# A two-layer attention and state-space block on one core: the front, gate, skip and second layer norm of all four items of a tile one step later

## What is computed

```python
# layer 0: attention between 4x4 blocks of pixels
x = x + attention(group_norm(x))
# layer 1: layer norm, a selective state-space scan on 4 chunks of 128 channels, layer norm, projection
xn = layer_norm(group_norm(x))            # 4096 positions, 512 channels
for chunk in 4 chunks of 128 channels:    # the "items" below
    xi, z = split(chunk @ in_proj.T)      # 256 + 256
    xc = silu(causal_conv4(xi) + conv_b)
    dt, B, C = split(xc @ x_proj.T)       # 8, 16, 16
    dt = softplus(dt @ dt_proj.T + dt_b)
    for position: h = exp(dt*A)*h + (dt*xc)*B ; y = sum_s h*C   # 16 states
    y = (y + xc*D) * silu(z)
    out_chunk = y @ out_proj.T + skip*chunk
out = x + layer_norm(all chunks) @ proj_w.T + proj_b
```

## Time and profile before

| what | value |
|---|---|
| median of 3 runs | 16086.48 us (16082.97 to 16089.99) |
| the profiled execution's own time | 16090.54 us |
| its span | 16088.7 us, mean granted clock of PE 0.947 |
| DVE busy | 14823.6 us (92%) |
| POOL busy | 14788.2 us (92%) |
| PE busy | 14186.2 us (88%) |
| ACT busy | 11509.9 us (72%) |
| windows 2, 3, 4, 5 of one ordinary tile (around 8.6 ms) | 61.74, 61.85, 58.54, 60.26 us |

### The profile page before, as it was taken

How to read it: one execution, slowest core, us unless ns; L and a number is a source line. 1 busy time by engine, 2 the same in 40 slices (tenths; PEclk the granted TensorE clock), 3 DMA queues, 4 the chain that set the end, 5 groups by cost and what they waited for, 6 DMA issues and landing times. The chain is left out here.

```text
span 16088.7 us, 151421 instructions
## 1 busy us (share of the span) xinstructions
PE 14186.2 (88%) x30720; PEld 5741.6 (36%) x30720; DVE 14823.6 (92%) x13024; ACT 11509.9 (72%) x18891; POOL 14788.2 (92%) x6275
## 2 busy tenths in 40 slices
PE   6988989889898898888889888899888898888888
PEld 2333333333333333333333333333333333333333
DVE  6999999999999999999999999999999999999998
ACT  5777767777677767777677776777767777677776
POOL 5999989999899989999899998999989999899998
PEclk8999999999999999999999999999999999999999
DMA  3444444444444444444444444444444444444444
GB/s 131 156 163 163 159 153 162 162 164 153 157 157 160 163 155 158 159 160 169 150 156 162 157 169 149 158 163 161 163 148 161 164 160 166 150 153 164 156 154 139
DMA packets 739082, 2537.63 MB, mean 158 GB/s; under 512 B 77241, under 2 KB 78017, under 8 KB 721729
## 3 DMA queue, kind: packets, MB, share of 16 engines
q1 hardware_dynamic: 738112, 2527.45, 46.1%
HBM read 2376.15 MB, written 150.99 MB: 157 GB/s over the span
## 5 line engine op out<-in xcount | busy, mean ns | idle before, releaser
L1460 POOL TENSOR_TENSOR RING<-RING,CS 128x1024 f32<-128x1024 f32 x4096 | 9597.9, 2363 | 1036.2 <-DVE RING L1150 973.3
L1150 DVE TENSOR_TENSOR_SCAN RING<-DA,HS,RING 128x512 f32<-128x512 f32 x8192 | 9946.1, 1265 | 496.9 <-ACT DA L777 451.1
L388 PE MATMUL YP<-RING,EYE 128*128 128x512 f32 x16384 | 8172.0, 632 | 1400.6 <-POOL RING L1460 1307.3
L777 ACT ACTIVATE DA<-ITEM,AN 128x512 f32<-128x512 f32 x8192 | 5495.8, 684 | 3017.5 <-DVE RING L1150 3001.5
L388 PEld LDWEIGHTS YP<-RING,EYE 128*128 128x128 f32 x16384 | 3126.8, 198 | 5995.0 <-issue 3596.3
L1130 DVE TENSOR_TENSOR RING<-DTP,BS 128x1024 f32<-128x1024 f32 x3072 | 3687.7, 1205 | 129.0 <-ACT DTP L847 117.6
L1447 POOL TENSOR_TENSOR RING<-ITEM,BS 128x1024 f32<-128x1024 f32 x1024 | 2421.3, 2365 | 10.0 <-DMA BS<-bc_rows 0.3
L388 PE MATMUL FL<-XN,WC 128*128 128x512 f32 x4096 | 1913.9, 611 | 9.8 <-ACT XN L866 4.6
L388 PEld LDWEIGHTS FL<-XN,WC 128*128 128x128 f32 x4096 | 821.4, 201 | 1087.4 <-issue 1079.1
L791 ACT ACTIVATE ITEM<-FL,COL 128x512 f32<-128x512 f32 x512 | 348.9, 682 | 1056.8 <-PE FL L388 1056.6
L388 PE MATMUL FL<-LS,WP 128*128 128x512 f32 x2048 | 983.2, 603 | 6.1 <-POOL LS L1482 6.1
(11 more groups left out here) (125 smaller groups left out, 10879.3 us busy)
## 6 DMA issues: line engine op xcount, KB each, us to landing
BS<-bc_rows SPq DMA_DIRECT2D x2048, 512.0 KB, 4.9
CS<-bc_rows SPq DMA_DIRECT2D x2048, 512.0 KB, 3.6
XR<-in_x SPq DMA_DIRECT2D x128, 1024.0 KB, 7.6
x_slices<-XR SPq DMA_DIRECT2D x64, 1024.0 KB, 8.3
XR<-x_slices SPq DMA_DIRECT2D x64, 1024.0 KB, 7.6
out<-XR SPq DMA_DIRECT2D x64, 1024.0 KB, 8.1
XR<-in_wqkv SPq DMA_DIRECT2D x24, 1024.0 KB, 7.8
bc_rows<-ROWS SPq DMA_DIRECT2D x256, 64.0 KB, 4.5
```

Source lines behind the costliest of these rows:

```text
L388: return pe.matmul(*a, **k)
L777: act.activation(DA[:, h, :], DT[:, i % 2, h, :], ACT.Exp, scale=AN[:, h, s:s + 1]).then_inc(dA_ready, 1)
L1150: dve.tensor_tensor_scan(H[:, slot(n), h, :], DA[:, h, :], U[:, slot(n), h, :], HS[:, i % ITEMS, h, s:s + 1], ALU.mult, ALU.add).then_inc( ...
L1460: pool.tensor_tensor(G[:, slot(n)], H[:, slot(n)], CS[:, s % C_ROWS, :].unsqueeze(1).broadcast_to([P, NH, T]), ALU.mult).then_inc(g_ready, 1)
```

## The change

d becomes 1 in every window. The two places that used d for another purpose keep their behaviour: `xi_first` stays at step 15 of the window before, except in window 3 and the `new` window (`conv_late`). The calls that did not go by d but touch the same PSUM banks are moved one step along with it: on PE the means of the second layer norm (window 4, steps 7 and 8 to 8 and 9) and the first block of the last projection (window 5, steps 6 and 7 to 7 and 8); on DVE the centring of the second layer norm (step 9 to 10) and the first `finish` (step 8 to 9). Whatever is at `s == k + d` moves on each engine: PE's second half of the convolution, z, dbc, both dt matmuls, the out projection and window 2's means; ACT's copies, silus, softplus pieces, group norm, square and rstd of the first layer norm; DVE's gate, skip, centring and scaling of the first layer norm, and the order of U 5 and 7; POOL's four dt operations. Not moved: ACT's skip term (12), `dtx_copy` (15), the square (11) and rstd (15) of the second layer norm, PE's d term (9), SP's queue.

```diff
         def late(j, new=False):
-            return 1 if j == 3 or new else 0
+            return 1
+
+        def conv_late(j, new=False):
+
+            return j == 3 or new
...
                     if front:
-                        if s == 0 and d:
+                        if s == 0 and conv_late(j, new):
                             front_left(tile, w)
...
                     if j == 0 and ln2:
-                        if s == 7:
+                        if s == 8:
                             pe.wait_ge(yb_ready, tile * ITEMS + w)
                             channel_mean(YB, mu2_ready, (0, 1))
-                        if s == 8:
+                        if s == 9:
                             channel_mean(YB, mu2_ready, (2, 3))
...
                     if j == 1 and ln2:
-                        if s == 6:
+                        if s == 7:
                             pe.wait_ge(yn_ready, ahead)
                             pe.wait_ge(yb_ready, tile * ITEMS + w)
                             proj(0, (0, 1))
-                        if s == 7:
+                        if s == 8:
                             proj(0, (2, 3))
...
-                    if j == 0 and ln2 and s == 9:
+                    if j == 0 and ln2 and s == 10:
                         centre(YB, mu2_ready, cen2_ready, ahead)
                     if j == 1 and ln2:
-                        for at, o in ((8, 0), (11, 1), (13, 2), (15, 3)):
+                        for at, o in ((9, 0), (11, 1), (13, 2), (15, 3)):
```

## The result

The changed kernel takes 16385.29 us (16379.01 to 16385.95, 4 runs) against 16084.72 us (16072.48 to 16089.99, 4 runs): the ratio is 1.0187, 95% interval 1.0169 to 1.0205. It is 300 us slower. The prediction was 16,110 us with a range of 16,045 to 16,185.

A forecast was written before the change was run, and what follows sets the result against it. DVE and POOL, each 92% busy, bound it by turns; only POOL's idle time counts. Window 4 +62, window 2 +25, special and first windows -63 make +24 on 16090.5, less 4.1 to the runs' median: 16,110 us, range 16,045 to 16,185.

The forecast's parts named there:

- slower, 0.40: Whole kernel: chance 0.40 that the change measures slower, against 0.45 same and 0.15 faster; a measurement tells 0.2%, 32 us.
- The gate's wait vanishes, the stall moves to scan 5: Early windows: DVE's gate wait for PE, 473 us, falls under 30; scan 5 waits instead, at +20.94 against +20.82.
- +18.67 without the gate's wait: Window 4 before the change: scan 5 would start 18.67 us after scan 0, not +20.82, if the gate did not wait.
- Window 4, +1.1: POOL's waits up to out 11 sum to 3.9 against 2.7 before; +1.1 us in each of 56 windows, +62.
- Window 5, 0: POOL is always behind DVE there and waits for nothing, so scan 5 coming 1.5 earlier is worth 0.
- over 150: Sign that the forecast is right: DVE waits for `dtx_copy` in over 150 windows.
- Window 2, +0.7: POOL waits 1.5 at out 10 against 0.80 before: +0.7 us in each of 35 windows, +25.
- Window 3, unchanged: Window 3 is unchanged and inherits the delay, since its convolution waits for out 14; priced at 0.
- The special windows, -57: Per image: tile 4's window 5 -4.4, the next +1.2, tile 5's window 5 with attention window -4.0, tile 6's window 4 -1.0.
- Slower by PE: Rival, chance 0.13: PE, nearly full in window 5, can't catch up; 57 windows 2 lose 1.5 each, +85, 16,195 us.
- Faster: z not held: Rival, chance 0.12: the gate does not hold z, or silu finds it ready; scan 5 1.2 earlier, -80, some 16,005 us.
- The C rows: Rival, chance 0.08: a C row lands 0.7 late at outs 7 to 10 in 64 windows 5, +45, 16,155 us.

The follow-up runs named there:

- e1: Changed kernel, but in windows 2, 4, 5 PE issues z before sum 0 instead of behind it: 16118.53 us, ratio 1.0021 to the kernel before.
- e7: Kernel before with one edit, PE issues the convolution's second half one step later, behind sum 15: 16165.61 us, ratio 1.0049 to the kernel before.
- e4: Changed kernel with z ahead of sum 0 and POOL's dt operations at their old steps, in windows 2, 4, 5: 15992.32 us, ratio 0.9946.
- e3: Changed kernel with POOL's four dt operations back at their old steps in windows 2, 4, 5: 16242.02 us, ratio 1.0103 to the kernel before.
- e2: Changed kernel with two extra matmuls on PE ahead of sum 0 in windows 2, 4, 5, result overwritten by z: 16300.91 us, ratio 1.0135.
- e12: Changed kernel with extra unread matmuls in ordinary windows 2, four ahead of sum 12 and five ahead of sum 13: 16379.79 us, ratio 1.0185.

## Why the prediction was wrong

The direction that I thought possible (slower, 0.40) came true, the size did not: +300 where +24 stood, outside the range.

Two steps failed. The length of sum 0 was taken from a row in which PE had hardly been idle, and put into windows where PE idles 2 us before it (window 5, 0 forecast, +49). And window 3 was put at nothing because its code is unchanged (+83): POOL's dt*x, moved behind out 12, was weighed against DVE's wait for its copy and not against PE's sums and the convolution behind them. The special windows, put at -57 (+36), met the slow sum 0 as well, lost more to z's order than was forecast, and have a part that stays open. Term by term:

**The gate's wait vanishes, the stall moves to scan 5.** Right in window 4, in place and size: 473.2 to 4.6 us, and scan 5 at +20.94 to +20.97 in all 49 ordinary windows 4. e1 shows that z behind sum 0 is what holds scan 5, as the prediction read it. Its "+18.67 without the gate's wait" is not right: the front's chain would have held scan 5 at about +19.5 (rows under e7, and e4's +19.49).

**Window 4, +1.1.** Measured 96.3 / 56 = +1.7. The waits of POOL at outs 6 to 11 are 3.96, as forecast, and the term was still 0.6 short. In the window shown the 1.78 can be counted: POOL's idle time grew by 1.38 (2.85 to 4.23, the second handover before a U included), the length of its operations by 0.14, and the next scan 0 comes 0.26 later behind POOL, after a wait of 0.77 for `dtx_copy` that the window did not have. The forecast had called that copy covered in such windows by POOL's queue; DVE waited for it all the same (and in fewer places than the "over 150" under its signs: 123 waits, 162.8 us, against 64 and 117.6 before). POOL's order is 1.0 to 1.1 us of a window 4 (60.36 to 59.30 in e3's undisturbed ones, 59.13 to 58.17 from e1 to e4), more than the +96 less +67 of e3 suggests.

**Window 5, 0.** This step failed. "Always behind DVE, waits for nothing" was read off a row in which scan 5 came at +22.4; the forecast put the new form at +20.9, 1.5 earlier. It came at +22.6 in 26 of 35, because z started 3.29 after sum 0 instead of 1.81. The prediction took the length of sum 0 and z from one late window, in which PE had been idle 0.69 before sum 0. In the windows changed it is idle 2.0 to 2.3, and there scan 5 came past +22 in 51 of 127. e2 took that out and window 5 went back to 60.26.

**Window 2, +0.7.** Over the 50 windows of the table 32 us were measured where 19 stood (25 less the 6 of the first windows). That this is near is luck: the clock adds 34 of them (e2), which I did not have, and without it the windows 2 cost nothing (-2).

**Window 3, unchanged.** The largest miss, +83 us. The prediction said only that it inherits the delay. It inherits more: the dt*x of window 2, moved behind out 12, and the U behind it hold the sums ahead of window 3's convolution, PE idles 4.6 and 3.3 us, and they run at half clock, so that the convolution starts 1.9 later, and the window is 1.9 longer. e3 (POOL's old order) takes back 45 us and e12 (PE kept busy there) 67, two ways into one chain. The prediction did count the dt operations' move against DVE's wait for the copy, and not against PE's sums.

**The special windows, -57.** They were to gain and lost 36. Window 5 of tile 4 gained 2.9 instead of 4.4 and the window after it lost 4.2 instead of 1.2; window 5 of tile 5 with the attention window after it lost 2.0 instead of gaining 4.0; window 4 of tile 6 lost 1.8 instead of gaining 1.0. In window 5 of tile 4 the clock is the whole miss (64.89 on the mean as changed, 63.24 in e2, where 67.76 less 4.4 is 63.36); in the window after it z's order is the whole loss but 0.7 us (63.69 to 60.23 in e1, 59.49 before). z ahead turns the group to -20, both orders to -47. With them the gain is there, but these are other kernels than the one forecast. In the attention window itself (69.79 before, 75.57 after) POOL's order is 2.3 of the 5.8, z's 0.7 (74.89), both 3.4 (72.20); the rest stays open.

**The rivals.** "Slower by PE" expected PE to fall behind in window 5 by being full. Its sign showed (window 5 over 61), but PE was slow there for the opposite reason, that it had stood idle. "Faster: z not held" would have needed e1's order. The C rows had hardly a part: POOL's waits for them are 35.8 us, 29.8 before.

By size, from the runs: z's order, with the clock that it meets, 267 us; of these the clock at the gate 84; POOL's order 143. Both together are 393, 17 less than the sum, which is inside the intervals; some 37 of POOL's 143 are the clock's as well (e3). What the late form is worth without the two is e4's own result, 0.54% or 87 us.

What stays open: what decides whether sum 0 behind 2.0 us of idle time is slow, and the rest of the attention window's loss.

## What to carry to other kernels

A wait that goes away is worth only what the chain beside it leaves: follow the next operation to its own inputs before pricing it, and check that the edit that removes the wait does not push that chain (e7, one condition, took 438 us of the wait away and was 80 us slower; in e4 the gate waits as little, nothing stands in the front's way, and it is 87 us faster). When an edit moves work past an instruction that waits, put ahead of that wait whatever doesn't need it: PE's z before sum 0 was worth 267 us here, because PE, waiting for the gate, held up the z queued behind and in 51 of 127 windows came back at half clock. Price a matmul by a row that had the same idle time in front of it, and check the windows that the diff does not touch.

## What the hardware showed that I had not expected

TensorE takes 1.88 to 1.98 us for the four matmul rows of most sums (some 3640 of 4096 in the changed kernel) and up to 3.8 for the others, with values between where the clock changes within a sum. An idle time of 2.27 us after a convolution was enough for a slow one (3.50), in an engine that is 87% busy over the span. The granted clock is 1.00 in some stretches (8859 to 8864) and 0.50 in others (8720 to 8728). The Trainium skill, "TensorE: Matmul & The Clock Gate", Part 1: The HAM clock gate, says that in the three kernels that it measured the gate was at one of two levels only, half and full. The trace agrees; the 0.72 above is the mean of a stretch that holds both. The idle time right in front does not decide it alone: behind 2.00 us the sum took 1.98, behind 2.02 us 3.46, and behind 2.63 (sum 13 of window 2 before the change) 1.98.

Keeping TensorE busy with matmuls that nobody reads gained 84 us (e2). But the penalty can move: e12 removed it in one window (-67 us) and found it in the next (+58 us), with a mean granted clock over the span of 0.954 against 0.936, and no time saved. The mean clock is no measure of what it costs.
